# Expert rows of six groups brought by GpSimd: a plain and an accumulating transfer into one buffer, in place of one plain transfer and two VectorE adds

## What is computed

```python
# h: residual rows, xf = layernorm(h), 4096 rows of 256
topw, topi = top_k(softmax(xf @ router_w), 2)        # two of eight experts per row
routed = sum over the two of topw * (silu(xf @ w1[e]) @ w2[e])
shared = sigmoid(xf @ shared_gate_w) * ((silu(gate) * up) @ shared_down)
out = h + routed + shared
```

## Time and profile before

| | |
|---|---|
| runs | 1019.66, 1021.77, 1019.19 us (median 1019.66) |
| profiled execution | 1021.38 us, of which the span is 1019.6 us |
| TensorE busy | 98% of the span, VectorE 72%, ScalarE 64%, GpSimd 52% |
| mean granted TensorE clock | 0.996 |
| tiles end, TensorE starts `hidden(3)` | 968.44 us |
| last matmul | 1015.2 us |

### The profile page before, as it was taken

The page is one execution under the profiler, slowest core; times in us unless marked ns, Lnnn a source line. Parts: engine busy times, 40 slices in busy tenths (PEclk is TensorE's granted clock), DMA queues, the critical chain, the costliest instruction groups (busy, mean ns, idle before and its releaser), DMA issues.

```text
span 1019.6 us, 23069 instructions
## 1 busy us (share of the span) xinstructions
PE 998.7 (98%) x7994; PEld 867.1 (85%) x7994; DVE 735.9 (72%) x1912; ACT 651.9 (64%) x1924; POOL 527.9 (52%) x574
## 2 busy tenths in 40 slices
PE   9989999999999999999999999999999999999988
PEld 7878888888888888888898889888887889999977
DVE  4867785786788578857858885786677676766666
ACT  5678883775677477747846884786577465555421
POOL 0045633556456455735555564557245498555543
PEclk9999999999999999999999999999999999999999
DMA  9120000101100010100011000101104727666387
GB/s 309 43 49 1 2 2 1 43 1 44 42 1 23 22 42 2 43 22 22 7 39 42 1 27 17 43 1 44 42 1 172 248 91 217 194 206 183 116 279 232
DMA packets 42583, 74.30 MB, mean 73 GB/s; under 512 B 8183, under 2 KB 27415, under 8 KB 42471
## 3 DMA queue, kind: packets, MB, share of 16 engines
q1 hardware_dynamic: 33671, 47.62, 14.3%
q0 software_dynamic: 8496, 25.18, 7.6%
q10 hardware_dynamic: 304, 0.03, 0.0%
HBM read 40.28 MB, written 32.52 MB: 71 GB/s over the span
## 4 chain that ended last, share of the span: by engine, by line
PE 80%; DVE 7%; ACT 2%; DMA 2%; issue 2%; SPq 0%; POOL 0%; POOLq 0%; DVEq 0%; ACTq 0%
PE proj_ps L73 11%; PE proj_ps L75 11%; PE proj_ps L74 11%; PE pT_ps L817 11%; PE proj_ps L830 10%; PE s_ps L799 9%; PE s_ps L73 2%; PE s_ps L75 2%; PE s_ps L74 2%; PE proj_ps L1091 2%; PE proj_ps L1092 2%; PE proj_ps L1086 1%; PE s_ps L1046 1%; DMA back<-expert_out_rows 1%; PE pT_ps L1076 1%
## 5 line engine op out<-in xcount | busy, mean ns | idle before, releaser
L1142 ACT ACTIVATE prob<-s_ps,nmax 128x255 f32<-128x255 f32 x512 | 238.3, 480 | 137.9 <-DVE nmax L1352 137.0
L1862 POOL TENSOR_SCALAR prob<-prob,rinv 128x255 f32<-128x255 f32 x128 | 138.4, 1081 | 254.0 <-DVE rinv L1370 253.5
L1352 DVE TENSOR_REDUCE nmax<-s_ps 128x2 f32<-128x510 f32 x256 | 159.3, 680 | 22.4 <-PE s_ps L799 21.8
L817 PEld LDWEIGHTS pT_ps<-ident,prob 128*128 128x128 f32 x1024 | 114.8, 140 | 32.6 <-issue 24.2
L817 PE MATMUL pT_ps<-ident,prob 128*128 128x128 f32 x1024 | 136.5, 276 | 0.0
L830 PE MATMUL proj_ps<-probT,v 128*64 128x256 f32 x1024 | 124.9, 386 | 0.4 <-DVE probT L1377 0.4
L1864 POOL TENSOR_SCALAR prob<-prob,rinv 128x255 f32<-128x255 f32 x128 | 119.4, 933 | 0.0
L1359 DVE TENSOR_TENSOR qk_space<-proj_ps,qk_space 128x512 fp32r<-128x512 f32 x128 | 87.7, 685 | 33.4 <-ACT qk_space L1154 33.0
L1149 ACT ACTIVATE prob<-prob,rinv 128x255 f32<-128x255 f32 x128 | 67.1, 524 | 66.4 <-DVE rinv L1370 66.3
L799 PE MATMUL s_ps<-qk_space 64*128 64x256 f32 x1536 | 108.3, 287 | 0.4 <-DVE qk_space L1359 0.4
L1142 ACT ACTIVATION_READ_ACCUMULATOR prob<-s_ps,nmax 128x1 f32 x512 | 108.6, 212 | 0.0
(11 more groups left out here) (275 smaller groups left out, 2681.5 us busy)
## 6 DMA issues: line engine op xcount, KB each, us to landing
xg<-expert_in_rows SPq DMA_DIRECT2D x71, 130.0 KB
back<-expert_out_rows SPq DMA_DIRECT2D x6, 1024.0 KB, 15.8
xin<-in_x_dram SPq DMA_DIRECT2D x8, 512.0 KB, 4.6
z_columns<-z2T_hi SPq DMA_DIRECT2D x8, 512.0 KB, 2.6
z_columns<-z2T_lo SPq DMA_DIRECT2D x8, 512.0 KB, 3.7
out_dram<-resid SPq DMA_DIRECT2D x7, 448.0 KB
z3T_hi<-z_columns POOLq DMA_DIRECT2D x5, 512.0 KB, 5.0
z3T_lo<-z_columns POOLq DMA_DIRECT2D x5, 512.0 KB, 4.8
```

The lines of the kernel that those rows point to most:

```text
L817: m = pe.transpose(pT_ps[h][:, o:o + P], prob[u_par(u)][:, h, qt, kt * P:(kt + 1) * P], ident[:])
L1142: m = act.activation(prob[u_par(u)][:, h, qt, 1:N], s_ps[b][h][:, qt * N + 1:(qt + 1) * N], ACT.Exp, bias=nmax[b][:, n:n + 1], accum_out=r ...
L1352: dve.tensor_reduce(nmax[b][:, 2 * h:2 * h + 2], s_ps[b][h][:].rearrange("p (q k) -> p q k", q=2)[:, :, 1:N], AX_X, ALU.max, negate=True). ...
L1862: pool.tensor_scalar(prob[k][:, 0, 1, 1:N], prob[k][:, 0, 1, 1:N], rinv[k][:, 1:2], None, ALU.mult).then_inc(s_nA1, 1)
```

## The change

SyncE's `load_back` is gone. GpSimd issues, for each of the groups 2 to 7, a plain transfer of the first expert's rows into `back[g][:, 1]` and, once that has landed (a wait on GpSimd), an accumulating transfer of the second expert's rows onto the same place. The transfers go in pairs of groups, put between the low parts and `add_experts`. VectorE adds `back[g][:, 1]` once, with a wait for both transfers.

```diff
-            def load_back(g):
-                sp.dma_start(back[g][:].rearrange("p k t d -> p k (t d)"),
-                             y_rows[0:TOP * ROWS, :].rearrange("(k n p t) d -> p k n (t d)", k=TOP, p=P, t=GT)[:, :, g, :]
-                             ).then_inc(s_back[g], 16)
...
-            for k in range(SLOTS):
-                sp.wait_ge(s_yst[k], 16 * len(range(k, RUN, SLOTS)))
-            for g in range(ADDED_BY_DMA, GROUPS):
-                load_back(g)
...
-            def add_second(g):
+            def add_both(g):
                 rows = resid[:, GT * g:GT * g + GT, :]
-                dve.wait_ge(s_back[g], 16)
+                dve.wait_ge(s_back[g], 16 * TOP)
                 if g < EXPERTS_FIRST:
                     dve.wait_ge(s_added, 2 * g + 2)
                 else:
                     dve.wait_ge(s_woe, 2 * g + 2 + FREE_W)
-                dve.tensor_tensor(rows, rows, back[g][:, 1], ALU.add).then_inc(s_first, 1)
-
-            def add_first(g):
-                rows = resid[:, GT * g:GT * g + GT, :]
-                dve.wait_ge(s_first, g + 1 - ADDED_BY_DMA)
-                dve.tensor_tensor(rows, rows, back[g][:, 0], ALU.add).then_inc(s_all, 1)
+                dve.tensor_tensor(rows, rows, back[g][:, 1], ALU.add).then_inc(s_all, 1)
 
             product(3, 0)
             product(3, 1)
             product(4, 0)
-            add_second(2)
             product(4, 1)
-            add_first(2)
-            add_second(3)
-            add_first(3)
+            add_both(2)
+            add_both(3)
             product(5, 0)
-            add_second(4)
             add_shared(3)
             product(5, 1)
-            add_first(4)
+            add_both(4)
             add_shared(4)
             product(6, 0)
-            add_second(5)
             product(6, 1)
-            add_first(5)
+            add_both(5)
             add_shared(5)
-            add_second(6)
             product(7, 0)
-            add_first(6)
             product(7, 1)
-            add_second(7)
+            add_both(6)
             add_shared(6)
-            add_first(7)
+            add_both(7)
             add_shared(7)
...
+            def bring(g, k):
+                rows = y_rows[ROWS * k + GR * g:ROWS * k + GR * (g + 1), :].rearrange("(p t) d -> p (t d)", t=GT)
+                both = back[g][:, 1].rearrange("p t d -> p (t d)")
+                if k:
+                    pool.wait_ge(s_back[g], 16)
+                    pool.dma_start(both, rows, accum_op=ALU.add).then_inc(s_back[g], 16)
+                else:
+                    pool.dma_start(both, rows).then_inc(s_back[g], 16)
+
             hidden_split_lo(3)
             for k in range(SLOTS):
                 pool.wait_ge(s_yst[k], 16 * len(range(k, RUN, SLOTS)))
             for g in range(ADDED_BY_DMA):
                 add_experts(g, 0)
+            for g in range(2, 4):
+                bring(g, 0)
             hidden_split_lo(4)
+            for g in range(2, 4):
+                bring(g, 1)
+            for g in range(4, 6):
+                bring(g, 0)
             hidden_split_lo(5)
+            for g in range(4, 6):
+                bring(g, 1)
+            for g in range(6, GROUPS):
+                bring(g, 0)
             for g in range(ADDED_BY_DMA):
                 add_experts(g, 1)
             hidden_split_lo(6)
+            for g in range(6, GROUPS):
+                bring(g, 1)
             hidden_split_lo(7)
```

## The result

The kernel after takes 1035.34 us (median of 4, 1034.35 to 1037.82) against 1020.71 for the kernel before in the same comparison: a ratio of 1.0146, interval 1.0127 to 1.0165. The change makes it slower by 14.6 us. Forecast were 1035.2 and 15.5 us more.

A forecast was written before the change was run, and what follows sets the result against it. TensorE was taken as bound, losing time only in a 3.21 us hole and the half clock behind it. Three serial accumulating round trips make the last add 15.5 us late: 1019.66 plus 15.5 gives 1035.2, range 1025 to 1046.

The forecast's parts named there:

- What bounded the kernel before: TensorE's one hole, 3.21 us before `shared_rows(4)`, as `add_shared(3)` queued behind `add_second(4)`'s wait for a late transfer.
- half clock: TensorE at 0.50 (1.2 GHz) behind the hole before `shared_rows(4)`; put at 1.2 us.
- The ring and the three round trips: GpSimd's low parts need VectorE's products behind its adds, so three accumulating trips run in series; 7.5 and 9.9 us per pair.
- step 2: `bring(2, 1)` leaves at 988.0; group 2 is in at 995.5, group 3 at 997.9.
- step 4: `bring(4, 1)` leaves at 1004.3, group 4 in at 1011.8, `shared_rows(5)` starts at 1014.0: 13.1 us late.
- This decides: The added chain of plain landing, GpSimd wait, accumulating landing and add sets the time: last add 15.5 us late.
- The adds at nothing: Six VectorE `add_first` taken away, 1.22 us each, 7.3 us, counted as winning nothing by themselves.
- GpSimd's issues at nothing: Twelve added issues on GpSimd, 9.5 us, mostly covered by idling; counted at nothing, 2 us at most.
- Occupation: Six blocks turned from plain to accumulating add 7.5 us of full occupation on the transfer engines.
- Accumulating costs no more than plain: Rival: 4.9 us for each trip with waits still in a ring, giving 1024; chance 0.07.
- Short round trips: Rival: group 3 in by 988.1, so TensorE no later; about 1018, chance 0.06; landed before 984.7, faster by more, 0.03.
- The rule of the Trainium skill: Transfers on GpSimd's queue take 3.2 us for 512 KB, no accumulating surcharge; whole change near 1018, a small chance.

The follow-up runs named there:

- experiment 9: Kernel before with VectorE's `add_shared(3)` and `product(5, 1)` moved ahead of `add_second(4)`: 1016.60 us, ratio 0.9968.
- experiment 5: Kernel after, plain transfers into separate halves, no GpSimd wait: same places 1027.49 us; all twelve at once 1026.22; those ahead of the first `add_experts` 1024.14.
- experiment 2: Kernel after with all six plain transfers issued early and all six accumulating ones behind the low parts of group 4: 1033.34 us.
- experiment 3: Kernel after with the plain pair 2/3 ahead of the first two `add_experts`, and these behind the accumulating pair 2/3: 1034.43 us.
- experiment 4: Kernel after with VectorE's `product(5, 0)` and `product(5, 1)` moved ahead of `add_both(2)`: 1033.29 us.
- experiment 8: Kernel before with the six `add_first` left out: 1019.59 us against 1019.58, ratio 1.0007.
- experiment 7: Kernel after with plain halves issued by SyncE at once, GpSimd only accumulating, pair 2/3 first: 1026.81 us, ratio 1.0070.
- experiment 1: Kernel after with the second transfer into each buffer plain instead of accumulating, waits and places kept: 1031.47 us, ratio 1.0112.

## Why the prediction was right

**What bounded the kernel before** was right in place and near in size: hole 3.2 plus half clock 1.2 makes 4.4 us, and the reordered kernel won 2.9 by the medians (experiment 9) and 4.8 by the tail. The half clock was read too small: the prediction's own lines, 4.4 us against 2.8 for `shared_rows(4)`, make it 1.6.

**The ring and the three round trips** are in the trace, at the places named. Their sizes, in T+, against the steps of the prediction (its clock less 968.44) and the trace of after (less 966.86):

| step | predicted | measured |
|---|---|---|
| 2: `bring(2, 1)` leaves; group 3 in | 19.6; 29.5 | 18.9; 26.9 |
| 3: `shared_rows(4)` starts (before: 22.6) | 32.4 | 29.6 |
| 4: `bring(4, 1)` leaves; group 4 in | 35.9; 43.4 | 32.8; 38.2 |
| 4: `shared_rows(5)` starts (before: 32.4) | 45.6 | 40.5 |
| 5: `bring(6, 1)` leaves; group 6 in | 49.8; 57.3 | 46.0; 54.0 |
| 6: last add ends (before: 47.8) | 63.4 | 61.8 |

Two terms were sized too large: the accumulating pair of step 2 took 8.0 us from first issue to second landing, not 9.9, and the single trip of step 4 took 5.33, not 7.5. Three were too small. From group 4's landing to the issue of `bring(6, 1)` it took 7.8 us, not 6.4, because `product(6, 1)` waited 1.18 us for ScalarE's `silu`. Behind the last hole `shared_rows(7)` ran at half clock, which I had left to the range: it took 4.6 us (1023.20 to 1027.76) instead of the 2.8 counted. And the stores behind the last add took 3.9 us, not 3.3. The errors partly cancelled, so that the forecast came so close (15.5 against 14.6) is in part luck.

**"This decides"** was too simple. The prediction laid all 15.5 us on the waits in series. Taken apart one edit at a time, the 14.6 us are, by the tail and in brackets by the medians: 3.6 (2.7) accumulating, 3.3 (4.0) the wait for the first landing on GpSimd, 3.4 (1.3) the places behind the low parts, 2.3 (2.6) the two accumulating transfers that stood ahead in the queue. The last 2.0 (4.1) stay in the kernel with twelve plain transfers ahead, and there they are late stores, not a late add (experiment 5). These parts hold for this order of taking away, the tails come from one execution each, and the intervals of neighbouring kernels overlap. What is clear of noise is that the wait, the places and the queue's order together cost time (12.0 to 4.1 us longer than before by the medians, with the intervals well apart); that accumulating by itself does is not, though the trace has each such transfer at half the rate. Experiments 2, 3 and 4 show that they are no independent sum: relieving one group's transfer gave 0.2 to 1.7 us of tail, since the next came late in its place. What the first two holes cost is the queue's order as much as any latency.

**The adds at nothing** was right within 0.3% (experiment 8). **GpSimd's issues at nothing** holds for the kernel after, where the next low parts were not yet due; with twelve in a row it does not (experiment 5). **Occupation**, 7.5 us of new work for the transfer engines, was put at nothing on the path, with 2 or 3 us for late stores left to the range. Experiment 7, without the waits, shows 2.9 us of late stores and 1.3 us before them.

**The rivals.** "Accumulating costs no more than plain" was priced at 1024 (its own terms, 1.4 late and twice some 2 more, make 1025); the run that has its condition took 1031.5. The step that failed is its 4.9 for each trip. Group 2's first plain half, behind two accumulating transfers in the queue, was in 9.6 us after its issue (977.50 to 987.07), and group 3's second took 7.0 us, from 988.29 to 995.28. So the price of its mechanism, not the mechanism, was wrong. Short round trips did not occur in the kernel after: its transfers into `back` took 5.3 to 10.9 us from issue to landing.

The rule of the Trainium skill (page "DMA: Bandwidth & Descriptors", section "Anatomy of one DMA — SWDGE (gpsimd) path", the fit of 2.0 us plus bytes over 436 GB/s, 3.2 us for 512 KB) is below every one of them; it is stated for one transfer, and says nothing of others in the same queue or of accumulating. Another page of the Trainium skill, "Collectives: The Full Stack", section "The bandwidth ceiling: the fold count and why AG ≠ RS ≠ AR", says that a ReduceScatter moves at half the rate of an AllGather because its add needs two source reads. For the accumulating transfers here the trace has the same ratio, 197 to 209 GB/s against 406 to 414; whether the reason is the same no run shows.

## What to carry to other kernels

An addition moved from an engine into the transfers is worth only what that engine's time was worth at the spot, here nothing, and it is paid with twice the occupation, a second landing in series and a place in GpSimd's list. Before such a change, read for whose result the late instruction's static queue holds up something that is already complete: here one line moved won what the additions could not. And when a queue works in order and is full, moving one transfer ahead is a loan from the next; measure at the end, not at the hole. Then look behind the last add too: what had been lent here came due in the list of stores.

## What the runs showed of the hardware

- How long TensorE runs at half clock (0.50, 1.2 GHz) after a restart does not follow from how long it idled. After 4.50 us idle (experiment 7, restart at 990.25) it ran so for 2.9 us, after 4.60 (experiment 3, restart at 1007.29) for 5.8. First two windows of the former, then three of the latter, of 2 us each:

```profile
990.00:992.00 2.00, 1.75 (x8) 1.78 (x9) 1.49 (x4) 0.95 (x2) 1.28 (x1) 0.50 1.06 251
992.00:994.00 2.00, 2.00 (x14) 2.00 (x14) 0.00 (x0) 0.15 (x1) 1.77 (x2) 0.71 1.06 245
```

```profile
1008.00:1010.00 2.00, 2.00 (x12) 2.00 (x11) 0.82 (x2) 1.11 (x2) 0.73 (x1) 0.50 0.92 295
1010.00:1012.00 2.00, 2.00 (x11) 2.00 (x11) 1.91 (x3) 0.63 (x1) 1.41 (x2) 0.50 1.10 217
1012.00:1014.00 2.00, 2.00 (x10) 1.72 (x10) 1.47 (x4) 0.00 (x0) 2.00 (x3) 0.73 1.02 201
```

- After 10.27 us idle (kernel after) it was 2.8 us, after 9.98 (experiment 4) 3.8, after 10.80 (experiment 1) 5.9 and after 14.50 (experiment 2) 5.7. All eighteen restarts of these traces after 2.42 us idle or more began at 0.50; in sixteen the clock rose after 2.8 to 5.9 us, in two the 5.5 us of work left were over first. The four restarts after 0.95 to 2.23 us began at 1.00. What sets the time within that range stays open.
- VectorE's 128x1024 add from two buffers took 1.22 us alone and up to 3.06 beside GpSimd's low parts. In the kernel before:

```profile
982.82 2.31 DVE L1792 TENSOR_TENSOR resid<-resid,back 128x1024 f32<-128x1024 f32 x1
```

```profile
982.51 1.54 POOL L1927 TENSOR_TENSOR h_lo<-h_full,h_hi 128x512 fp32r<-128x512 f32 x1 [2.44 <-ACT h_hi L1246]
```

The low part ends at 984.05, 1.23 us after the add's start, and the add lasts about that much longer than alone, less 0.14. The add of 3.06 us fits too: it began at 986.38, and the low parts ended at 988.35, 1.97 us later. It looks as if the add only began its work when GpSimd's instruction was through. The Trainium skill, page "SBUF — State Buffer", section "Who interferes with whom", says that a VectorE instruction with two SBUF inputs contends with a GpSimd instruction that reads SBUF; the rows agree.
